# Folding the own level into the tree nodes, an argmax with tokens on partitions, and running sums by a triangular product, in one fused two-layer kernel

## What is computed

```
# first layer, experts
logits = xt @ Wg.T                              # 8 per token
top1   = argmax(logits)                         # ties: the first expert
y      = sum over e of (top1 == e) * (gelu((xhat*s_e + b_e) @ W1_e + b1_e) @ W2_e + b2_e)

# second layer, attention (16 heads, level(t,s) = 0 if s == t, else floor(log2(s XOR t)) + 1)
cg    = cumsum(A * softplus(x @ Wdt.T + dt_bias))          # over the 512 tokens
decay = exp(cg_t - cg_s)  for s <= t
Lam   = softplus(Lp * (x @ Wdl.T))                         # per token, head and level
Wmat  = (Q K^T / 8) * decay * Lam[t, h, level(t,s)]
o     = (Wmat @ V) @ Wout.T + x ; layer norm of o
```

## Time and profile before

| | us |
|---|---|
| median of 3 runs | 1280.03 (1277.32 to 1282.98) |
| the profiled execution | 1280.37 |
| its span, first to last instruction | 1278.6 |

### The profile page before, as it was taken

The page is one execution under the profiler, slowest core; times in us unless marked ns, Lnnn a source line. Parts: engine busy times, 40 slices in busy tenths (PEclk is TensorE's granted clock), DMA queues, the critical chain, the costliest instruction groups (busy, mean ns, idle before and its releaser), DMA issues.

```text
span 1278.6 us, 18053 instructions
## 1 busy us (share of the span) xinstructions
PE 1113.7 (87%) x5756; PEld 672.1 (53%) x5756; DVE 1025.3 (80%) x2156; ACT 693.6 (54%) x1366; POOL 310.5 (24%) x197
## 2 busy tenths in 40 slices
PE   5789889898998989899898989989898998989872
PEld 3455546455564645556464555646555464546541
DVE  4588796978879697896969789696978969698577
ACT  3383745637375573736547373664737466373662
POOL 0050220504114050411405032140503205040183
PEclk9799989999999999999999999999999999999896
DMA  3000000000000000000000000000000000001226
GB/s 127 8 9 9 1 17 9 16 8 0 16 8 16 8 16 8 0 16 8 16 8 16 8 0 16 8 16 8 16 8 0 16 8 16 8 9 34 89 83 206
DMA packets 32563, 28.65 MB, mean 22 GB/s; under 512 B 1568, under 2 KB 26144, under 8 KB 32288
## 3 DMA queue, kind: packets, MB, share of 16 engines
q1 hardware_dynamic: 32544, 28.42, 6.7%
HBM read 16.09 MB, written 12.32 MB: 22 GB/s over the span
## 4 chain that ended last, share of the span: by engine, by line
PE 43%; DVE 43%; issue 11%; ACT 2%; DMA 1%; DVEq 1%; SPq 0%; POOLq 0%; POOL 0%; ACTq 0%
PE p L461 6%; DVE ms L1252 5%; DVE skip L1084 4%; PE p L623 3%; PE p L585 3%; DVE pair L1319 3%; DVE nodesT L1261 3%; DVE pair L1332 2%; DVE pair L1326 2%; PE p L476 2%; PE p L478 2%; PE p L477 2%; PE p L432 2%; DVE y L1164 2%; PE p L574 2%
## 5 line engine op out<-in xcount | busy, mean ns | idle before, releaser
L1521 POOL TENSOR_TENSOR pair<-pair,cgt 128x2048 f32<-128x2048 f32 x16 | 58.4, 3651 | 839.9 <-DVE pair L1319 839.9
L857 ACT ACTIVATE gx<-p 128x512 f32<-128x512 f32 x256 | 140.6, 593 | 10.1 <-PE p L478 8.5
L476 PE MATMUL p<-x1Th,Gl 128*128 128x512 f32 x256 | 120.0, 469 | 2.8 <-ACT gx L857 2.8
L817 ACT ACTIVATE gelu<-p,bias_u 128x512 f32<-128x512 f32 x32 | 22.0, 687 | 155.0 <-PE p L423 155.0
L478 PE MATMUL p<-x1Th,Gh 128*128 128x512 f32 x256 | 101.8, 398 | 0.0
L477 PE MATMUL p<-x1Tl,Gh 128*128 128x512 f32 x256 | 101.7, 397 | 0.0
L1534 POOL TENSOR_TENSOR vp<-vdw,beta 128x384 f32<-128x384 f32 (+3 forms) x80 | 80.8, 1043 | 56.0 <-DVE beta L1311 56.0
L393 PE MATMUL p<-xnT,MC 128*128 128x512 f32 x64 | 43.3, 768 | 58.4 <-DVE y L1157 58.4
L548 PE MATMUL p<-gx,x1T 128*32 128x512 f32 x512 | 79.6, 699 | 11.1 <-DVE pair L1336 10.3
L585 PEld LDWEIGHTS p<-vbd,pair 128*128 128x128 f32 x512 | 61.9, 191 | 43.0 <-issue 29.4
L1252 DVE TENSOR_TENSOR ms<-lam,K 128x64 f32<-128x64 f32 (+4 forms) x80 | 83.4, 1118 | 0.0
(11 more groups left out here) (239 smaller groups left out, 2742.4 us busy)
## 6 DMA issues: line engine op xcount, KB each, us to landing
xin<-in_x SPq DMA_DIRECT2D x16, 256.0 KB, 2.8
hx_scratch<-vdw SPq DMA_DIRECT2D x16, 256.0 KB, 2.5
res_scratch<-res SPq DMA_DIRECT2D x15, 256.0 KB, 2.0
W<-in_weights SPq DMA_DIRECT2D x1, 1477.5 KB, 9.5
gx<-hx_scratch SPq DMA_DIRECT2D x5, 256.0 KB, 4.0
out<-gx SPq DMA_DIRECT2D x5, 256.0 KB, 2.7
gx<-in_weights SPq DMA_DIRECT2D x1, 1216.0 KB, 11.9
GT<-hx_scratch SPq DMA_DIRECT2D x4, 256.0 KB, 3.7
```

What stands on the lines that cost most here:

```text
L476: pe.matmul(head_bank(h)[:, :], tile(Gl, h), x1Th[:, :], start=True, stop=False)
L857: act.activation(tile(gx, h, T), head_bank(h)[:, :], ACT.Copy).then_inc(R["gx_copied"], 1)
```

## The change

1. **Own level into the nodes.** `self_lam`, POOL's `own_level` and the addition in `pair_weights` go. A token's own Lam is written instead as a combination of node vectors: new `fold_own` on DVE (three operations, between `lam_sum` and `delta`) changes the per-level factors, `node_lams` multiplies by `member` (1 in every node that holds the token) instead of by the right half, and a copy fills node 31. `left` is changed once in the setup, by new `node_vectors` in `stages(None, 0)`, about 17 small DVE operations.
2. **Argmax with tokens on partitions.** `logits` makes four products with 8 columns; `top1` is five operations on 128 partitions by 32 (the last 96) columns and moves up to right behind `token_rows`; PE turns the one-hot by four transposes (new `turn_choice`, behind `gate_z(j, 0)`) and ACT writes `oh_b` and `mask_b` between its tanh and its gelu.
3. **Running sums.** `gates_to_rows`, `sums` and `sums_to_tokens` go; `running_sums` on PE makes them by four accumulating products with a triangular matrix `upto` and with ones.

```diff
@@ PE
+            def turn_choice(j):
+                pe.wait_ge(R["top1_steps"], 5 * j + 5)
+                pe.wait_ge(R["ch1_ready"], j + 1)
+                for n in range(TILES):
+                    mm = pe.transpose(P0[0][0:24, 128 * n:128 * n + 128], tile(oh, n, 3 * E), ident)
+                mm.then_inc(R["ohT_ps"], 1)
             def gate_u(j, q):
-                pe.wait_ge(R["top1_steps"], 7 * j + 7)
                 if q == 0:
-                    pe.wait_ge(R["ch1_ready"], j + 1)
+                    pe.wait_ge(R["mask_ready"], j + 1)
...
+            def running_sums(i):
                 pe.wait_ge(R["g_ready"], i + 1)
-                for n in range(TILES):
-                    mm = pe.transpose(P1[1][0:16, 128 * n:128 * n + 128],
-                                      dts[:, 576 + 16 * n:576 + 16 * n + 16], ident)
-                mm.then_inc(R["gT_ps"], 1)
...
+                g = dts[:, 576:640]
+                pe.matmul(P1[2][:, 0:64], upto[:, :], g, start=True, stop=False)
+                for n in range(1, TILES):
+                    mm = pe.matmul(P1[2][:, H * n:64], spread(ones[:, 0:1], [128, 128]), g[:, 0:64 - H * n],
+                                   start=False, stop=(n == TILES - 1))
                 mm.then_inc(R["cgT_ps"], 1)
@@ ACT, in gates0
+                act.wait_ge(R["ohT_ps"], j + 1)
+                act.activation(oh_b[0:24, :], P0[0][0:24, :], ACT.Copy)
+                act.activation(mask_b[0:8, :], P0[0][0:8, :], ACT.Copy, scale=BIG, bias=-BIG).then_inc(R["mask_ready"], 1)
@@ DVE
+            def top1(j):
+                lg = view(P0[2][:, 0:TILES * E], "p (n e) -> p n e", e=E)
...
+                dve.tensor_tensor(val, eq, spread(k("rank").unsqueeze(1), [128, TILES, E]), ALU.mult)\
                     .then_inc(R["top1_steps"], 1)
...
+            def fold_own(i):
+                dve.wait_ge(R["lam_ready"], i + 1)
+                if later(i):
+                    dve.wait_ge(R["nodes_ready"], i)
+                l = view(lam[:, :], "p (m l) -> p m l", l=LEVELS)
+                own = view(lam_own[:, :], "p (m l) -> p m l", l=6)
+                dve.tensor_tensor(own, spread(l[:, :, 0:1], [128, 64, 6]),
+                                  spread(own_coef[:, :].unsqueeze(1), [128, 64, 6]), ALU.mult).then_inc(R["own_steps"], 1)
+                dve.tensor_tensor(l[:, :, 1:6], l[:, :, 1:6],
+                                  spread(rbit[:, :].unsqueeze(1), [128, 64, 5]), ALU.mult).then_inc(R["own_steps"], 1)
+                dve.wait_ge(R["own_steps"], 2 * i + 2)
+                dve.tensor_tensor(l[:, :, 1:6], l[:, :, 1:6], own[:, :, 0:5], ALU.add).then_inc(R["lamx_ready"], 1)
...
             def pair_weights(i, n):
...
-                dve.tensor_tensor(tile(pair, n, 512), tile(pair, n, 512), tile(self_lam, n, 512), ALU.add)\
-                    .then_inc(R["lams_ready"], 1)
@@ DVE stages
-                    sums(i)
                     token_sums(i)
                     token_rows(i)
                 if j is not None:
-                    turn_logits(j)
+                    top1(j)
                 if i is not None:
                     level_factors(i)
                     lam_sum(i)
+                    fold_own(i)
...
-                if j is not None:
-                    top1(j)
@@ POOL
-            def own_level(i):
...
                 level_values(i)
-                own_level(i)
```

More of the change, by code:

```diff
@@ L671, in stages @@
                     gate_z(j, 0)
+                    turn_choice(j)
                 if i is not None:
@@ L1044, in before @@
                 step(dve.tensor_copy(expert_b[:, :], k("expert", rows=32)))
-                step(dve.memset(oh[:, :], 0.0))
                 step(dve.memset(ones[:, :], 1.0))
+                step(dve.tensor_tensor_scan(upto[:, :], spread(ones[:, 0:1], [128, 128]), ident, 0.0, ALU.mult, ALU.add))
+                at, width = cat["rank"]
+                for p in (32, 64, 96):
+                    step(dve.tensor_copy(K[p:p + 32, at:at + width], k("rank", rows=32)))
                 dve.wait_ge(R["setup_ps"], 2)
@@ L1063, in before, with node_vectors, step @@
                 dve.wait_ge(R["setup_done"], 3)
+            def node_vectors():
+                steps = [0]
+                def step(ins):
+                    steps[0] += 1
+                    ins.then_inc(R["basis"], 1)
+                    dve.wait_ge(R["basis"], steps[0])
+                step(dve.transpose(left_t[:, :], k("left")))
+                step(dve.tensor_reduce(member[:, :], view(left_t[:, :], "p (c n) -> p n c", c=4), AX.X, ALU.add))
+                step(dve.tensor_tensor(member[:, :], member[:, :], k("right"), ALU.add))
+                at = 0
+                for level in range(5, 0, -1):
+                    count = CHUNK >> level
+                    step(dve.tensor_reduce(rbit[:, level - 1:level], k("right", at, at + count), AX.X, ALU.add))
+                    at += count
+                step(dve.memset(ones_to[:, 0:1], 1.0))
+                for level in range(1, 6):
+                    step(dve.tensor_tensor(ones_to[:, level:level + 1], ones_to[:, level - 1:level],
+                                           rbit[:, level - 1:level], ALU.mult))
+                step(dve.scalar_tensor_tensor(own_coef[:, 0:5], ones_to[:, 1:6], -2.0, ones_to[:, 0:5], ALU.mult, ALU.add))
+                step(dve.tensor_copy(own_coef[:, 5:6], ones_to[:, 5:6]))
+                left = view(k("left"), "p (c s) -> p c s", c=4)
+                step(dve.scalar_tensor_tensor(left, spread(k("own_chunk").unsqueeze(2), [128, 4, CHUNK]), k("diag", 31, 32),
+                                              left, ALU.mult, ALU.add))
             def heads_low_part():
@@ L1132, in top1 @@
[L1132 to L1135, removed]
-                dve.transpose(ohT[:, :], oh[:, :]).then_inc(R["ohT_ready"], 1)
-                dve.wait_ge(R["ohT_ready"], j + 1)
-                if later(j):
-                    dve.wait_ge(R["out0_ps"], j)
-                dve.tensor_copy(oh_b[:, :], ohT[:, :])
@@ L1472, in stages @@
                     heads_low_part()
+                    node_vectors()
                 if j is not None:
```

107 lines of the change are left out of this document (44 added, 63 removed).

## The result

The changed kernel takes **1289.51 us** (median of 4 runs, 1287.97 to 1290.03), the kernel before 1279.09 beside it: ratio 1.0075, 95% interval 1.0049 to 1.0101. It is slower by 10.4 us; the forecast was 1289. Its profiled execution took 1290.02 us with a span of 1288.0, 9.4 more than before.

A forecast was written before the change was run, and what follows sets the result against it. DVE sets the pace up to `scan_c`, through `scan_inputs`, PE after it; +1.03 us a stage. Sum 13.4 + 0.9 - 1.5 - 4.4 + 0.5 = +8.9 on 1280.37: 1289 us, range 1283 to 1296, chance 0.57.

The forecast's parts named there:

- Sums: Ahead of the copy cgt, four small PE products replace transposes and scan: the copy starts 1.49 us earlier.
- The lock: Before `scan_inputs`: DVE operations with two SBUF inputs stand until POOL's instruction ends; of 1.49 us only 0.29 is left.
- rival 1: Small operations of `top1` aren't held by POOL: `scan_inputs` moves +0.12 us, 1272 us in all, faster; chance 0.12.
- The fold: `fold_own`, between `lam_sum` and `delta` on the path to `scan_inputs`: 1.52 us in all, bounds 1.2 and 2.9.
- Rival 2: Short runs in `fold_own` cost twice: +1.4 us for each of 15 stages, 1310 us; chance 0.06.
- The transposes: `turn_choice`, four new PE transposes in the half of the stage that PE sets: taken as +0.4 us (0 to 0.8).
- From c1 to ps1: Second half of `scan_c` to `pair_scores(1)`: PE runs as before to the end of `node_matrices`; segment -0.33 us a stage.
- rival 4: Longer pauses draw a second low-clock stretch into the half that PE sets: +20 us on 13 stages, 1309 us; chance 0.05.
- First stage: Mask now needs z1, a tanh and two copies on ACT, +0.3 us, and the setup +0.2: +0.5.
- the cover I had counted on: Setup's `node_vectors` (4 us) lies in DVE's 6 us of waiting for `out0`; uncovered it would cost those 4.
- Stage 0: PE's idle before `scan_c` grows from 2.09 to 3.4 us; the clock may fall: 0.1 to 1.7, taken as +0.9.
- the last: Last stage: no `top1`; `norm2` takes 1.1 instead of 4.53 us, three waits on L1336 shrink by 0.75 each: -4.4 us.

The follow-up runs named there:

- the argmax split: Changed kernel with the last three operations of `top1` moved from behind the first two to behind `pair_weights(0)`: 1275.28 us, ratio 0.9973.
- the same reordering: DVE's `scan_inputs` moved ahead of `node_lams`: on the changed kernel 1225.96 us, ratio 0.9563; on the kernel before 1279.77 us, ratio 1.0015.

## Why the prediction was right, and where it was not

**Sums.** Right: x1 to cgt is 1.49 us shorter wherever `values` runs at the same clock (22.68 to 21.19, 20.98 to 19.49).

**The lock.** Right, and with it the main step of the forecast. The third operation of the argmax stood 3.44 us beside POOL's L1545; rival 1, that 32 columns are too few to be held, is out. The Trainium skill's rule (SBUF — State Buffer, "Who interferes with whom") says that of two such operations one waits for the whole of the other, whatever its size, and the 3.44 us agree. `lam_sum` came 0.30 nearer to the sums' start (forecast 0.29).

**The fold.** Right: 0.56, 0.48 and 0.49 us, and 1.50 by the run without it. Rival 2 is out. `delta` moved by +1.23 as forecast and c1 by +1.26 (forecast 1.32).

**The transposes.** Right: 0.44 by the run that doubled them (taken as 0.4).

**From c1 to ps1: wrong, by +0.77 us a stage.** The step "from there to the end of `node_matrices` PE runs as before" failed. PE did the same work at another clock. In 3 of the 13 stages the segment is 11.76, which is the forecast's 11.79; in the other 10 the low clock lasts longer and it is 12.63 to 12.96. That the wait ahead of c1 makes the low clock is shown by filling it. Its length is not what decides how long the low clock lasts: PE waits 4.35 us in all 13 stages, the argmax split has the same wait and 11.94 on the mean, and the sums alone wait 2.96 and reach 13.1. What does decide stays open. I had this as rival 4 and priced it as a second low stretch in another place, at 20 us. It was the existing stretch that varied: c1 to ps1 takes 10.12 us with the wait filled.

**`values`: not in the sum at all, worth -0.79 us a stage.** The trace of before had its 4.6 us in every stage, and I never asked what the four products cost at the full clock. The two clock terms have opposite signs and nearly cancel (-0.02 a stage). That they do is luck: the same two terms make some 8 of the 15 us by which the forecast of the folding alone was wide, and 11 of the 17 of the sums alone.

**First stage: +3.8 for +0.5.** The extra time is TensorE's clock again. Windows of PE in the changed kernel (us, busy, granted clock, DMA share, GB/s), where the kernel before has 1.00 in each:
```profile
20.00:24.00 4.00, 4.00 (x15) 0.51 0.00 0
24.00:28.00 4.00, 4.00 (x17) 0.50 0.00 0
28.00:32.00 4.00, 4.00 (x24) 0.50 0.01 4
32.00:36.00 4.00, 4.00 (x8) 0.50 0.00 0
```
The 20 small products of the folded heads in it (L364, x40) took 8.21 us instead of 4.39. In exchange the window from 40 to 48 us, 0.50 before, is at 1.00. In the run with the argmax alone the same stretch has 1.00, and its first x1 comes at 48.39 us instead of 56.53. The short products of the new `logits` alone are thus not the cause. Nor is it chance: the window from 24 to 32 us is at 0.50 in all eight kernels that have the three parts (the changed one and its variants), with the first x1 at 55.2 to 60.1 us, and at 1.00 in the other six, with 48.4 to 52.7. It takes the argmax with at least one of the other parts; why, stays open. The setup's `node_vectors` ended at 56.5 us and `out0` at 56.1, so the cover I had counted on was used up.

**Stage 0 (+2.9 for +0.9) and the last (-7.0 for -4.4).** In stage 0 cgt to c1 grew by 3.72 us and not by 2.81. The new copy that fills node 31 takes 0.22 us in most stages and 1.10 here, beside POOL's L1558:
```profile
92.45 1.10 DVE L1301 COPY ms<-lam_own 128x64 f32<-128x64 f32 x1
```
That is 0.9 of the 2.0 us; the rest is in the stretches around it (x1 to cgt -1.08, c1 to ps1 +0.26) and not explained further. In the last, `norm2` took 1.11 instead of 4.53, as forecast. The waits on L1370 are 0.43, 0.20 and 0.82 where those on L1336 were 1.28, 1.00 and 1.55, so 2.4 us went there (forecast 2.25), and the wait for `left_halves` went from 3.20 to 1.48:
```profile
1239.92 0.91 PE L531 MATMUL p<-vp,xn 128*128 128x384 f32 x2 [1.48 <-ACT rs L929]
...
1241.53 3.73 PE L545 MATMUL p<-rs,GT 128*128 128x120 f32 x32
...
1249.77 1.07 PE L559 MATMUL p<-gx,x1T 128*32 128x512 f32 x8 [0.43 <-DVE pair L1370]
1254.36 1.06 PE L559 MATMUL p<-gx,x1T 128*32 128x512 f32 x8 [0.20 <-DVE pair L1370]
...
1261.32 1.13 PE L596 MATMUL p<-vbd,pair 128*128 128x128 f32 x8 [0.82 <-DVE pair L1370]
```
From the last product of L531 to L545 it is 1.61 us (1239.92 to 1241.53), where before it was 3.48, a wait of 0.43 for `nodesT` and a product at the low clock among it: 1.9 us that I had not counted. With 1.7 and 2.4 that makes 6.0 of the 7.0. I did not test these two terms.

## What to carry to other kernels

Price a change by the segment between two waits, and give each segment two lengths, one for each level of TensorE's clock: here the levels lie 2.4 us a stage apart behind one wait and 1.7 behind another, and a shift of 0.44 us moved a segment by 0.5 us that it has no instruction in. Where a profile says that an engine waits, look at what stands in the other engine's queue ahead of the operation waited for and isn't needed by it; and look whether that queue has room behind it, since the same reordering brought 64 us in one kernel and nothing in the other. A small DVE operation with two SBUF inputs cost as much here as the POOL instruction that it met (3.44 us for 0.18 us of work), so its place in the queue counts, not its size.

## What the hardware showed that I had not expected

- **Useless products can pay.** Four more products of 512 columns in a wait of 4.35 us took 2.44 us a stage off what follows.
- **The clock in one place depends on work far from it.** `values` stands behind a wait of 1.98 us in every stage of the changed kernel and runs at 2.4 GHz in two of four stages, at 1.2 in the other two (stages of 77.2, 75.3, 75.2 and 76.0 us in turn, the third segment taking part in it). What decides between them I can't say from these traces: the wait is the same.
- **Equal kernels vary by more than most edits here.** The runs of one kernel lay up to 0.9% apart (1219.86 to 1230.24 us), about 6 times the 1.7 us of one stage's `values`, and their mean granted clock goes with it (0.969 in the shortest, 0.963 in the longest). An effect below that needs the segments, not the total.
